# Attention scores of a macaron block: eight products of 128 stationary columns become 32 products of 32 stationary columns, each with its own 32 output partitions

## What is computed

```
q = jnp.einsum('bse,edh->bsdh', x, Wq) + bq      # 32 features d, 32 heads h
k = jnp.einsum('bse,edh->bsdh', x, Wk) + bk      # 8 heads, repeated 4 times
v = jnp.einsum('bse,edh->bsdh', x, Wv) + bv
scores = jnp.einsum('bsdh,bseh->bsde', q, k) / np.float32(np.sqrt(D))
attn = jax.nn.softmax(scores, axis=-1)
out = jnp.einsum('bsde,bseh->bsdh', attn, v)
```

## Time and profile before

| | |
|---|---|
| median of 3 runs | 1314.02 us (1314.0 to 1318.34) |
| the profiled execution | 1314.43 us |
| its span, first to last instruction | 1312.6 us |
| PE busy | 1253.2 us (95%) |
| PE weight loads busy | 1077.6 us (82%) |
| DVE, ACT, POOL busy | 837.8, 411.5, 437.1 us |
| mean granted TensorE clock | 0.986 |

### The profile page before, as it was taken

One profiled execution on the slowest core, in us unless ns is written; L12 is line 12 of the kernel. 1 busy time (PEld: TensorE's weight loads), 2 busy tenths in 40 slices (PEclk: granted clock), 3 DMA queues, 4 the chain that ended last, 5 costly groups with the idle time before them and its releaser, 6 DMA issues.

```text
span 1312.6 us, 21943 instructions
## 1 busy us (share of the span) xinstructions
PE 1253.2 (95%) x8776; PEld 1077.6 (82%) x8776; DVE 837.8 (64%) x1177; ACT 411.5 (31%) x590; POOL 437.1 (33%) x548
## 2 busy tenths in 40 slices
PE   5999999999999798999999999999999999979998
PEld 4788888888888677888888888888888888858887
DVE  3643343334333267888888887878888875198886
ACT  3322222222221123444344344444344443211110
POOL 1225443544231733324323433333333200051321
PEclk9999999999999898999999999999999999989999
DMA  7132333233212244555555545545545555116774
GB/s 256 53 116 89 128 108 118 89 128 100 78 65 112 73 112 112 162 153 145 146 142 132 155 132 154 164 132 147 158 123 154 137 136 187 47 67 223 271 272 177
DMA packets 197605, 178.91 MB, mean 136 GB/s; under 512 B 141312, under 2 KB 163840, under 8 KB 197504
## 3 DMA queue, kind: packets, MB, share of 16 engines
q1 hardware_dynamic: 182624, 158.11, 39.8%
q10 hardware_dynamic: 14880, 19.40, 4.3%
HBM read 103.55 MB, written 73.92 MB: 135 GB/s over the span
## 4 chain that ended last, share of the span: by engine, by line
PE 86%; DVE 9%; DMA 2%; issue 1%; POOL 1%; ACT 1%; SPq 1%; DVEq 0%; POOLq 0%
PE ps_b L257 12%; PE ps_b L259 12%; PE ps_b L258 12%; PE ps_a L257 11%; PE ps_a L259 10%; PE ps_a L258 10%; PE ps_t L264 6%; PE ps_s L1283 4%; DVE probs L1041 3%; PE ps_s L271 3%; PE ps_s L273 2%; PE ps_s L1333 2%; DVE odd_lo L992 1%; PE ps_s L278 1%; DVE qkv_tok L1036 1%
## 5 line engine op out<-in xcount | busy, mean ns | idle before, releaser
L257 PE MATMUL ps_a<-w_hi,odd_hi 128*128 128x512 f32 x464 | 187.0, 403 | 0.0
L259 PE MATMUL ps_a<-w_hi,odd_lo 128*128 128x512 f32 x464 | 182.3, 393 | 0.0
L258 PE MATMUL ps_a<-w_lo,odd_hi 128*128 128x512 f32 x464 | 182.1, 392 | 0.0
L257 PE MATMUL ps_b<-proj_hi,y_hi 128*128 128x256 f32 (+1 forms) x512 | 177.9, 347 | 0.0
L259 PE MATMUL ps_b<-proj_hi,y_lo 128*128 128x256 f32 (+1 forms) x512 | 172.6, 337 | 0.0
L258 PE MATMUL ps_b<-proj_lo,y_hi 128*128 128x256 f32 (+1 forms) x512 | 172.0, 336 | 0.0
L567 POOL TENSOR_SCALAR f_out<-f_out,token_on 128x1024 f32<-128x1024 f32 x31 | 88.6, 2857 | 173.8 <-DVE f_out L896 173.8
L291 POOL TENSOR_TENSOR var_eps<-moments,eps 128x1 f32<-128x1 f32 x96 | 18.4, 192 | 364.1 <-DVE moments L287 364.1
L613 POOL TENSOR_TENSOR f_tmp<-f_tmp,mask 128x1024 f32<-128x1024 f32 x32 | 72.7, 2273 | 146.9 <-DMA f_tmp<-f_scratch 146.9
L259 PEld LDWEIGHTS ps_b<-proj_hi,y_lo 128*128 128x128 f32 x512 | 97.1, 190 | 10.8
L896 DVE TENSOR_TENSOR f_out<-ps_b,bias_a 128x512 f32<-128x512 f32 x30 | 20.7, 691 | 132.9 <-PE ps_b L259 132.9
(11 more groups left out here) (181 smaller groups left out, 2783.1 us busy)
## 6 DMA issues: line engine op xcount, KB each, us to landing
xa<-in_L_attn_x SPq DMA_DIRECT2D x32, 512.0 KB, 5.6
f_tmp<-f_scratch SPq DMA_DIRECT2D x32, 512.0 KB, 5.0
x_ring<-in_L_attn_x SPq DMA_DIRECT2D x32, 512.0 KB, 4.2
f_scratch<-f_out SPq DMA_DIRECT2D x31, 512.0 KB, 3.0
x_scratch<-x_ring SPq DMA_DIRECT2D x30, 512.0 KB, 3.3
late<-x_scratch SPq DMA_DIRECT2D x22, 512.0 KB, 6.7
qkv_scratch<-qkv_tok SPq DMA_DIRECT2D x32, 256.0 KB, 3.0
f_scratch<-f_out ACTq DMA_DIRECT2D x60, 128.0 KB, 3.5
```

What stands on the lines that cost most here:

```text
L257: pe.matmul(acc, hi[:, k, :], w_h[:, k, cols], start=(k == 0), stop=False)
L258: pe.matmul(acc, hi[:, k, :], w_l[:, k, cols], start=False, stop=False)
L259: last = pe.matmul(acc, lo[:, k, :], w_h[:, k, cols], start=False, stop=(k == KB - 1))
```

## The change

For each j, the one product of 128 stationary columns is replaced by four products of 32 stationary columns (those of one t), each with the same 128 moving columns as before, and each written to its own 32 partitions of the output. The numbers that result, their place in `ps_s`, and the one signal after the last product are the same.

```
                         k_blocks = k_diag[:, :].rearrange("p (r j e) -> p j r e", r=R4, e=D)
                         for j in range(J8):
-                            last = pe.matmul(ps_s[:, j * P:(j + 1) * P], q_diag[:, j * P:(j + 1) * P],
-                                             k_blocks[:, j, :, :], start=True, stop=True)
+                            for b in range(T4):
+                                at = j * P + b * D
+                                last = pe.matmul(ps_s[32 * b:32 * b + 32, j * P:(j + 1) * P], q_diag[:, at:at + D],
+                                                 k_blocks[:, j, :, :], start=True, stop=True)
                         last.then_inc(scores, 1)
```

## The result

The changed kernel is slower: a median of 1326.48 us (17 runs, 1320.1 to 1332.94) against 1314.17 us for the kernel before (17 runs, 1306.53 to 1320.15). The ratio is 1.0089, with a 95% interval of 1.0068 to 1.011; that is 11.7 us more, 8.9 to 14.5. The forecast was 1324.6.

The account below looks back on a forecast made before the run. PE's order was taken to bound the kernel. Thirty tiles at 0.33 us (9.9), plus 0.24 and 0.5 for two special tiles, gave 10.6 us over the profiled 1314.43, hence 1325.0, or 1324.6 us after the 0.41 median offset; range 1314 to 1340.

Parts of the forecast that it names:

- nothing covers the scores: Scores on PE: added time delays both PE's and DVE's branches equally; entry hidden only where PE waits ahead.
- The body: Scores block: 64 new records run in fours side by side, taking 1.78 us, the time of the old 16.
- Entry 0.10: Start of each tile's scores: going into the 32-column form costs 0.10 us.
- exit 0.20: End of each tile's scores: the product behind them begins 0.20 us later.
- the heads: Existing 32-column matmuls at line 257's block: 64 records take 0.89 us, 0.50 of array time and 0.39 overhead.
- The sum: All 32 tiles: 30 at 0.33 us give 9.9, plus two special tiles; together 10.6 us.
- 0.24 and 0.5: First tile and half-clock tile at 502 us: entry hidden, adding 0.24 and 0.5 us.
- Loads as the bound: Rival at the scores: 128-column loads set the old pace, so each block gets 0.56 us shorter; 1296 us, chance 5%.
- The argument from line 343: Against the loads rival: line 343's second matmul comes 0.107 us after its load starts, so the matmul sets that time.
- Blocking records: Rival at the scores: a product's two records block each other, block 3.90 us; 1381 us, chance 8%.
- No change to be seen: Rival: entry and exit overlap long neighbouring products, or DVE's wait swallows the exit; 1316 to 1320 with both, chance 12%.
- Part of the four streams: Rival at the scores: only part of the four streams runs at once; 1334 to 1345 us, chance 7%.

Follow-up runs that it names:

- adding time alone: Kernel before, with each tile's last score product done two times more in the old 128-column form; ratio 1.0112, 14.7 us more.
- one changed product: Kernel before, with only the first of a tile's eight score products written as four of 32 columns; ratio 1.0089, 11.7 us more.
- four visits: Kernel before, with score products of even j as four of 32 columns and odd j left at 128; ratio 1.0346, 45.5 us more.
- 64 columns: Kernel before, with each score product as two of 64 stationary columns, each to its own 64 output partitions; ratio 1.0066, 8.7 us more.
- two pairs of profiles: Kernel before and changed kernel, each profiled a second time without further change; the repeats' ratios to the kernel before are 1.0021 and 1.0086.
- two products in a row: Changed kernel, reordered so two products (four records) in a row go to each group of 32 output partitions; ratio 1.0094 to the kernel before.
- runs of eight: Changed kernel, reordered so eight products in a row go to the same 32 output partitions; ratio 1.1017 to the kernel before, 134 us more.
- runs of 8: Changed kernel, reordered so four products (eight records) in a row go to each group of 32 output partitions; 83 us more than the kernel before.

## Why the prediction was right, and where it was off

**What bounds the kernel, and that nothing covers the scores.** Shown by adding time alone: 14.3 us added in the blocks, 14.7 measured. The reason given, VectorE's line 1036 waiting for the product behind the scores, stays argued: the wait is in these profiles, but its length (12.6 us before, 17.8 in the change, 13.5 with time added) doesn't go with the time added.

**The body: 16 x 0.111 = 1.78 us, four side by side.** Right in kind, a little too high in size. From first to last score are 1.682 us: 15 fours and the first load and spread. A four is 0.109 apart, not 0.111, which is 16 x 0.002, 0.04 us less for a tile. This is the mis-sized term: block 0.293 more, against 0.33 forecast. It also explains why one changed product costs a little more (0.327) than eight (0.293): each further four gives back about 2 ns.

**Entry 0.10 and exit 0.20, read from the heads.** Entry is 318 - 228 ns, 0.09. At the exit, the second product behind begins 0.540 us after the last score's start, 0.348 before; with the same work in it, 0.19 more. One changed product, four visits and 64 columns all confirm that it is a price for each visit. The weight loads show where it arises. Before, the first load of the scores starts 0.22 us ahead of the first score, under the product ahead (683.11 and 683.33), and the load of line 257 is under the last scores. In the changed kernel each of the two starts only with its own matmul:

```profile
683.11 1.98 PEld L1283 LDWEIGHTS ps_s<-k_diag,q_diag 128*128 128x128 f32 x16
685.00 0.19 PEld L257 LDWEIGHTS ps_b<-proj_hi,y_hi 128*128 128x128 f32 x1
```

```profile
686.83 1.69 PEld L1285 LDWEIGHTS ps_s<-k_diag,q_diag 128*32 128x32 f32 x64 [0.35 <-issue]
688.71 0.19 PEld L257 LDWEIGHTS ps_b<-proj_hi,y_hi 128*128 128x128 f32 x1 [0.20 <-issue]
```

The Trainium skill, "TensorEngine Tiling (Array Packing)", section "Key Properties", says that a change of tiling mode drains the engine; these runs agree in that no load of the next form is brought forward across the change, and give the price, 0.33 us for a visit with its way back. Line 343 (64 columns) pays it in the kernel before: from the product ahead to its start are 0.32 us (417.87 to 418.19), from its last start to line 257 0.20 (418.35 to 418.55). But not every narrow matmul does, and why stays open. The cluster logits alternate between 64 and 128 stationary columns 0.12 us apart, without a price at each change:

```profile
736.25 0.28 PE L271 MATMUL ps_s<-odd_hi,cen 128*128 128x256 f32 x1
736.37 0.28 PE L273 MATMUL ps_s<-odd_lo,cen 128*64 128x256 f32 x1
736.48 0.28 PE L271 MATMUL ps_s<-odd_hi,cen 128*128 128x256 f32 x1
```

**The sum.** 30 tiles x 0.293 are 8.8 us. From the first score on, the first tile took 0.10 more and the third, at half clock, 0.26 and 0.41 in the two pairs of profiles, where the forecast has 0.24 and 0.5. Together these are some 9.2 us, against 10.6 in the forecast. Measured are 11.7 (8.9 to 14.5), so the blocks alone would do. Between the profiles the stretch from the fourth tile to the last grew by 12.5 and 11.0 us, of which 28 blocks are 8.2. The other 4.3 and 2.8 us go with longer waits of PE behind VectorE (of lines 264 and 271 behind line 992 and of the heads behind line 1050, together: 13.1 us before and 17.6 in the change, 13.6 and 16.1 in the second pair) and with a longer line 1041. That the longer line 1041 makes them is argued, not shown. The new form does not bring them by itself, since two products in a row has nothing left over, and they come without it, since with time added alone 5 us are left over and line 1041 has a mean of 2.17 us. It is 2.07 us where the block was not changed at all (the old form with half the moving columns). What sets it stays open; each of these is one profile. The forecast had no such term, and it was luck that its too large body filled part of the gap.

**The rivals.** *Loads as the bound* fell: at 128 moving columns matmul and load are equally long. With 64 it holds. The argument from line 343 was weak, though: 0.107 us are from a load's start to a matmul's, while its two matmuls start 0.16 apart (418.19 and 418.35). What shows the pace of the moving columns is that a four of the new form comes each 0.109 us with 128 of them and twice as fast with 64. *Blocking records*: excluded by the fours, and explained by the waiting places in each group. In "TensorE: Matmul & The Clock Gate", section "The mechanism", the Trainium skill has strict order without reordering; here the measurement differs: in runs of eight the next group's first record starts while three of the group before, which are earlier in the program, still wait (13 of 16 started). Within a group nothing speaks against the order. *No change to be seen*: excluded, the whole interval of the ratio lies above 1.005. *Part of the four streams*: excluded by the 0.109. The 79% that "TensorE: Matmul & The Clock Gate" of the Trainium skill, section "Measured speedup vs the span model", gives for three tiles of 512 moving columns does not show in these fours of 128; no run has 512.

## What to carry to other kernels

Ask what bounds the undivided form before dividing TensorE's array in column groups. Here cutting one product of 128 stationary columns into four that move the same 128 columns bought nothing and paid about 0.3 us for each visit; only with 64 moving columns, where the loads bound the undivided form, did it gain. Keep divided products together and count the visits. Order the products so that neighbours go to different groups: the same 32 products took 1.7 us when they took turns and 5.7 us in runs of eight. Read such a change from the distance between starts around the block, since the line's busy time stayed at 64.2 us and would have shown nothing.

## What was not expected of the hardware

A column group takes in about three waiting matmuls beside the running one, as far as the starts tell: runs of 4 records for each group cost 0.07 us over perfect turns, runs of 8 cost 2.37, runs of 16 cost 4.00. In float32, a load of 128 stationary columns and a matmul of 128 moving ones have the same pace, 0.11 us, so halving the moving columns of an undivided product changed its block by nothing (2.246 us both times), while the divided one fell from 2.539 to 1.686 us. Across a change of form the weight loads, too, start no earlier than the matmuls: the first load came 0.22 us ahead of its matmul in the old block and with it in the new one.
